# Self attention of a decoder layer: the products of exponents and values issued two key blocks at a time, with 16 slots for exponents

## The chip, the core and the metric

The kernel runs on one core of a Trainium2 chip. Its metric is the device time of one execution in microseconds; lower is better. The core has TensorE (PE in the profile; PEld is its weight load), VectorE (DVE), ScalarE (ACT), GpSimd (POOL) and SyncE (SP), which issues most transfers here. TensorE writes its results to PSUM, which has eight banks of 128 partitions by 512 words of fp32; a semaphore count tells another engine that a tile is ready, or that a bank is free again.

## What is computed

One decoder layer of a transformer on x with 4 sequences of 1024 tokens and 256 features: self attention, cross attention to 77 context rows, and a gated feed-forward network, each behind a layer norm and with a residual sum. The change touches self attention alone, 16 heads of 16 features with a causal mask:

```python
Qt = jnp.einsum('bqhf,hfg->bqhg', Q, W_cross)
scores_cross = jnp.einsum('bqhd,bkhd->bhqk', Qt, K)
K_mixed = jnp.einsum('hfg,bkhg->bkhf', M, K)
scores_conv = jnp.einsum('bqhf,bkhf->bhqk', Q, K_mixed)
scores = (gt * scores_cross + (1.0 - gt) * scores_conv) * scale
scores = jnp.where(causal[None, None], scores, -jnp.inf)
attn = jax.nn.softmax(scores, axis=-1)
out = jnp.einsum('bhqk,bkhd->bqhd', attn, V).reshape(b, s, H * hd)
```

## The kernel before

The stages follow one another: projections to q, k and v (to about 160 us), self attention (to about 646 us), its output projection and the query projection of cross attention, cross attention, and the feed-forward part (from about 900 us).

Self attention takes 16 groups, each of four heads of one sequence (HG is 4). In each group three kinds of work run on TensorE:

- **Maxima.** Scores with queries on partitions go into one of three PSUM banks (MXB), and VectorE reduces each tile to the largest value of each query. `ring` lists 38 such tiles and two small transposes: t0, which turns the maxima of the first half of the queries (place 15 of the ring), and t1, which turns those of the second half (place 39). These two write only 32 partitions. VectorE copies their result to a row, and a transfer adds it to the operands of the score tiles. The maxima of group g + 1 are made while the scores of group g are. In the text, r with a number is a place of the ring; r15 and r39 are called t15 and t39.
- **Scores.** With keys on partitions, in one of three other banks (STB). ScalarE takes the exponent of each tile and writes it to `prob`, a ring of NPS slots of 512 columns fp32. There are 38 such units in a group (NST), s0 to s37.
- **Products.** Exponents times values, fp32, for 128 keys (a key block) at a time: a set of four matmuls, one for each head, each from 128 partitions to 17 columns of the array (16 features and the sum of exponents). The profile has two records for each of these matmuls, so a set is x8. The sets are p0 to p11: p0 to p3 for the first 512 queries (4, 4, 2 and 1 score units; 512, 384, 256 and 128 query columns), p4 to p11 for the second 512 (five sets of 512 columns, then 384, 256 and 128). The first half accumulates in bank 6, the second in bank 7 (PVB).

The order of all this on TensorE is the list `plan`, made once from a few rules and the same in each group: a set is placed LAG = 3 score units behind the last unit that it needs; a set that would come behind s37 is placed in the next group's plan, with -1 (p10 behind s1 and p11 behind s2, for the group before). The maxima of the next group are spread evenly between the scores from s3 on. With t39 and r0 placed behind s3, the order before in one group is:

```
s0 s1 p10 s2 p11 s3 t39 r0 s4 r1 s5 r2 s6 p0 r3 s7 r4 s8 r5 s9 r6 s10 p1 r7 s11 r8 r9
s12 p2 r10 s13 p3 r11 s14 r12 s15 r13 s16 r14 s17 p4 t15 s18 r16 s19 r17 s20 r18 r19
s21 p5 r20 s22 r21 s23 r22 s24 r23 s25 p6 r24 s26 r25 s27 r26 s28 r27 s29 p7 r28 r29
s30 r30 s31 r31 s32 r32 s33 p8 r33 s34 r34 s35 r35 s36 r36 s37 p9 r37 r38
```

What waits for what: a score tile for the exponent three units back (`s_ex`, its bank); a tile of maxima for VectorE's work three places back (`s_mxe`); a product set for the exponent of its last unit (`s_ex`); an exponent for the product that frees its slot in `prob` (`s_pv`, against NPS); the copy of the first half's output for p3 and of the second's for p11 (`s_pv`), the first sets of a half (p0, p4) for the copy that frees their bank (`s_u`). VectorE works strictly in the order of the ring; behind the reduce of r10 and of r38 it has the two or three small operations that split the maxima into two bf16 parts (`parts_of_max`). In groups 5, 9 and 13 it also has `shares`, divisions for the sequence that is done, between r38 and t39. In the last group there are no maxima to make; the first steps of the next stage (`EARLY`) stand between its score units.

Of the kernel before, what the change touches and what calls it, by code (L numbers as in the profile page):

```python
# [23 lines left out]
def need(eng, semaphore, count):  # L24

    if count > 0:
        eng.wait_ge(semaphore, count)


def program(nc, x, ctx_t, mask_t, Wq, bq, Wk_t, bk, Wv_t, bv, Wo_t, bo, W_cross, shift_w, gate,  # L30
# [41 lines left out]
    with root:  # L72
# [505 lines left out]
        def self_plan():  # L578

            mx_units, st_units, sets = [], [], []  # L580
            for half in range(2):
                for r in range(4):
                    if half:
                        mx_units += [(half, 1, r, h, 1, 0, 512, False) for h in range(HG)]
                    hb = HG // (r + 1)
                    mx_units += [(half, 2 * half, r, h, hb, half * 512, (r + 1) * P, True)
                                 for h in range(0, HG, hb)]
            for half in range(2):
                for kt in range(4 * half + 4):
                    diag = kt >= 4 * half  # L590
                    q0 = (kt % 4) * P if diag else 0
                    n = 512 - q0
                    hb = max(1, (512 // n) // 2 * 2)
                    first = len(st_units)
                    st_units += [(half, kt, h, hb, q0, n, diag) for h in range(0, HG, hb)]
                    sets.append((half, kt, first, len(st_units), kt == 0, kt == 4 * half + 3, q0, n, hb))
            return mx_units, st_units, sets

        mx_units, st_units, sets = self_plan()
        NST = len(st_units)  # L600
        n_half = sum(1 for m in mx_units if m[0] == 0)
        half_end = [max(s[3] for s in sets if s[0] == h) for h in range(2)]
        ring = [("m", i) for i in range(len(mx_units))]
        ring.insert(n_half + 4, ("t", 0))
        ring.append(("t", 1))
        NMX = len(ring)
        NPS, LAG, LATE = 12, 3, 3
        MXB, STB, PVB = (0, 1, 2), (3, 4, 5), (6, 7)
        NMB, NSB = len(MXB), len(STB)

        plan, at = [], 0
        for u in range(NST):
            plan.append(("s", u, 0))
            plan += [("p", s, -1) for s, x in enumerate(sets) if x[3] - 1 == NST + u - LAG]
            plan += [("p", s, 0) for s, x in enumerate(sets) if x[3] - 1 == u - LAG]
            if u == LATE:
                plan.append(("r", NMX - 1, 0))
            upto = max(0, u - LATE + 1) * (NMX - 1) // (NST - LATE)
            plan += [("r", n, 1) for n in range(at, upto)]
            at = upto  # L620
# [161 lines left out]
        def self_tensor(t, first):  # L782
            def maxima(g, n):
                i, N = g % GB, g * NMX + n
                kind, m = ring[n]
                dst = bank[MXB[N % NMB]]
                if n == 0:
                    t.wait_ge(ld[i], 16 * NLD * (g // GB + 1))
                need(t, s_mxe, N + 1 - NMB)
                if kind == "t":  # L790
                    t.wait_ge(s_mt, 2 * g + m + 1)
                    nc.tensor.transpose(dst[0:32, 0:P // 2].bitcast(BF16),
                                        mt[:, m].rearrange("p t m -> p (t m)"), identb[:]).then_inc(s_mxf, 1)
                    return
                half, k, r, h0, hb, k0, w, diag = mx_units[m]
                for h in range(hb):
                    mm = nc.tensor.matmul(dst[:, h * w:(h + 1) * w],  # L797
                                          stq[i][0:R, half, h0 + h, r * P:(r + 1) * P],
                                          stk[i][0:R, h0 + h, k0:k0 + w],
                                          start=(h == 0), stop=not diag, skip_group_check=True)  # L800
                if diag:
                    mm = nc.tensor.matmul(dst[:, 0:hb * w].rearrange("p (h w) -> p h w", h=hb)[:, :, w - P:w],  # L802
                                          identb[:], tri_q[:, 0:hb], start=False, stop=True, skip_group_check=True)
                mm.then_inc(s_mxf, 1)

            def scores(g, u):
                i, U = g % GB, g * NST + u
                half, kt, h0, hb, q0, n, diag = st_units[u]
                if u == 0 or u == half_end[0]:
                    t.wait_ge(md[g % 2][half], 32 * (g // 2 + 1))  # L810
                need(t, s_ex, U + 1 - NSB)
                dst = bank[STB[U % NSB]]
                for h in range(hb):
                    mm = nc.tensor.matmul(dst[:, h * n:(h + 1) * n],  # L814
                                          stk[i][0:RM, h0 + h, kt * P:(kt + 1) * P], stq[i][0:RM, half, h0 + h, q0:q0 + n],
                                          start=(h == 0), stop=not diag, skip_group_check=True)
                if diag:
                    mm = nc.tensor.matmul(dst[:, 0:hb * n].rearrange("p (h n) -> p h n", h=hb)[:, :, 0:P],  # L818
                                          identb[:], tri_k[:, 0:hb], start=False, stop=True, skip_group_check=True)
                mm.then_inc(s_st, 1)  # L820

            def products(g, s):
                half, kt, first, end, fresh, last, q0, n, hb = sets[s]
                if fresh:
                    need(t, s_u, 2 * g + half - 1)
                t.wait_ge(s_ex, g * NST + end)
                for h in range(HG):
                    mm = nc.tensor.matmul(bank[PVB[half]][h * VW:h * VW + VC, q0:512], va[g % GB][:, kt, :, h],  # L828
                                          prob[:, (g * NST + first + h // hb) % NPS, (h % hb) * n:(h % hb + 1) * n],
                                          start=fresh, stop=last)  # L830
                mm.then_inc(s_pv, end - first)

            if first:
                for n in range(NMX - 1):
                    maxima(0, n)
                return

            t.wait_ge(s_set, GB)
            for g in range(G):
                for what, which, ahead in plan:  # L840
                    if g == G - 1 and what == "s" and which in EARLY:
                        if which == min(EARLY):
                            t.wait_ge(s_mxe, G * NMX)
                        EARLY[which](t)
                    if what == "s":
                        scores(g, which)
                    elif what == "p" and g + ahead >= 0:
                        products(g + ahead, which)
                    elif what == "r" and g + ahead < G:
                        maxima(g + ahead, which)  # L850
            for s, x in enumerate(sets):
                if x[3] - 1 > NST - 1 - LAG:
                    products(G - 1, s)


# [778 lines left out]
        with nc.Block() as block:  # L1634
# [26 lines left out]
            @block.tensor  # L1661
            def _(t):
                qkv_tensor(t)
                arrive(t)
                self_tensor(t, True)
                t.wait_ge(s_phase, 5)
                self_tensor(t, False)
# [177 lines left out]
```

## Time and profile before

| | us |
|---|---|
| median of three runs | 1145.98 (1141.55 to 1146.23) |
| the profiled execution | 1145.35 |
| its span, first to last instruction | 1143.6 |
| TensorE busy | 1044.8 |
| VectorE busy | 750.0 |
| ScalarE busy | 573.4 |
| TensorE busy within 165 to 646 us (481 us) | 478.15 |

The page of the profile gives busy time by engine, groups of instructions and releasers; the timeline gives single instructions or merged stretches in order. The end of a matmul record is modelled: it contains a tail that lies under the next one, so distances between starts tell more than durations. "Idle" in brackets behind a row is the time that the engine stood before it, and what ended it.

### The profile page before, as it was taken

The numbers are of one execution on the slowest core, as the hardware profiler recorded it, in microseconds if no ns is written. First come the engines' busy times: TensorE is split into PE (matmuls) and PEld (weight loads), VectorE is DVE, ScalarE is ACT, GpSimd is POOL, SyncE is SP. The second block draws the span as 40 slices with busy tenths as digits, with TensorE's granted clock in tenths as the row PEclk, the third lists the DMA queues.
The fourth block names the chain that finished last, engine by engine and source line by source line (L and its number), as shares of the span: only waits on it lengthen the run. The fifth ranks groups of instructions, "written<-read, shape, count | busy, mean of one in ns | idle before, by whom it ended". The sixth has DMA issues, their size and how long they took to land. (4 is left out here: it accounts for less than half of the span.)

```text
span 1143.6 us, 19037 instructions
## 1 busy us (share of the span) xinstructions
PE 1044.8 (91%) x7092; PEld 602.9 (53%) x7092; DVE 750.0 (66%) x1603; ACT 573.4 (50%) x1043; POOL 230.8 (20%) x192
## 2 busy tenths in 40 slices
PE   2889789999999999999999878898599899999997
PEld 2777234444444444444444455444243588888886
DVE  5997877777888878877785266555254355555552
ACT  1454146667767767667676549356256311111110
POOL 6654630000000000000000057200100133333331
PEclk9999679999999999999999998899699899999999
DMA  7279833433334444444110166666653201111101
GB/s 242 103 228 262 225 59 70 75 76 71 75 61 87 89 85 87 89 88 85 40 62 23 59 192 185 145 140 144 150 134 99 99 18 47 47 57 56 56 20 37
DMA packets 89636, 113.48 MB, mean 99 GB/s; under 512 B 13819, under 2 KB 74747, under 8 KB 88008
## 3 DMA queue, kind: packets, MB, share of 16 engines
q1 hardware_dynamic: 85896, 107.25, 37.6%
q10 hardware_dynamic: 3648, 5.02, 2.2%
q8 instruction: 56, 0.92, 0.4%
q14 instruction: 36, 0.29, 0.1%
HBM read 66.26 MB, written 45.45 MB: 98 GB/s over the span
## 5 line engine op out<-in xcount | busy, mean ns | idle before, releaser
L774 ACT ACTIVATE prob<-bank 128x512 f32<-128x512 f32 (+1 forms) x608 | 329.3, 575 | 184.8 <-PE bank L818 106.0
L726 DVE TENSOR_REDUCE pm<-bank 128x1 f32<-128x512 f32 (+3 forms) x608 | 364.6, 656 | 83.8 <-PE bank L802 63.7
L797 PE MATMUL bank<-stk,stq 96*128 96x512 bf16 (+3 forms) x768 | 227.3, 340 | 8.4 <-DVE pm L726 4.1
L814 PE MATMUL bank<-stq,stk 98*128 98x512 bf16 (+3 forms) x768 | 222.9, 329 | 0.9 <-ACT prob L774 0.8
L828 PE MATMUL bank<-prob,va 128*17 128x512 f32 (+3 forms) x1536 | 164.5, 501 | 0.0
L797 PEld LDWEIGHTS bank<-stk,stq 96*128 96x128 bf16 x768 | 70.2, 99 | 160.3 <-DVE pm L726 115.6
L1550 ACT ACTIVATE e_sg<-bank 128x512 f32<-128x512 f32 x48 | 28.7, 598 | 188.4 <-PE bank L132 188.4
L1308 ACT ACTIVATE xprob<-bank 80x512 f32<-80x512 f32 x128 | 73.8, 593 | 87.1 <-PE bank L1345 83.8
L957 POOL TENSOR_TENSOR c_rstd<-c_ve,mhalf 128x4 f32<-128x4 f32 x8 | 8.1, 1008 | 508.0 <-DVE c_ve L125 508.0
L814 PEld LDWEIGHTS bank<-stq,stk 98*128 98x128 bf16 x768 | 69.4, 98 | 56.9 <-issue 12.4
L1270 DVE TENSOR_REDUCE xpm<-bank 128x4 f32<-128x320 f32 x128 | 60.5, 489 | 53.8 <-PE bank L1331 52.1
L802 PE MATMUL bank<-tri_q,identb 128*128 128x128 bf16 (+2 forms) x352 | 88.6, 252 | 0.0
L818 PE MATMUL bank<-tri_k,identb 128*128 128x128 bf16 (+2 forms) x352 | 86.5, 246 | 0.0
L132 PE MATMUL bank<-e_xnt,wg 128*128 128x512 f32 x288 | 76.7, 402 | 1.4 <-DVE e_xnt L1511 1.4
L1479 POOL TENSOR_TENSOR e_ht<-e_hf,e_ht 128x512 fp32r<-128x512 f32 x48 | 62.4, 1300 | 73.1 <-DVE e_ht L1506 73.1
L132 PE MATMUL bank<-e_xnt,wu 128*128 128x512 f32 x288 | 73.8, 392 | 0.0
L132 PE MATMUL bank<-wd,e_ht 128*128 128x256 f32 x576 | 70.5, 283 | 3.2 <-POOL e_ht L1479 3.2
L132 PEld LDWEIGHTS bank<-wd,e_ht 128*128 128x128 f32 x576 | 70.1, 192 | 4.2 <-POOL e_ht L1479 3.6
L1504 DVE TENSOR_TENSOR e_hf<-bank,e_sg 128x512 f32<-128x512 f32 x48 | 33.1, 690 | 50.6 <-ACT e_sg L1550 50.6
L828 PEld LDWEIGHTS bank<-prob,va 128*17 128x17 f32 x1536 | 31.4, 117 | 57.0 <-ACT prob L774 33.8
L132 PEld LDWEIGHTS bank<-e_xnt,wg 128*128 128x128 f32 x288 | 54.2, 191 | 12.7 <-DVE e_xnt L1511 1.8
L132 PEld LDWEIGHTS bank<-e_xnt,wu 128*128 128x128 f32 x288 | 54.6, 190 | 11.7
(173 smaller groups left out, 1388.6 us busy)
## 6 DMA issues: line engine op xcount, KB each, us to landing
qk<-a_parts SPq DMA_DIRECT2D x32, 384.0 KB, 4.1
od<-u_out SPq DMA_DIRECT2D x16, 512.0 KB, 3.2
oin<-od SPq DMA_DIRECT2D x32, 256.0 KB
od<-xu SPq DMA_DIRECT2D x16, 512.0 KB, 2.7
xq<-c_parts SPq DMA_DIRECT2D x16, 384.0 KB, 3.1
xstq<-xq SPq DMA_DIRECT2D x32, 192.0 KB, 3.9
stq<-qk SPq DMA_DIRECT2D x28, 192.0 KB, 4.9
stk<-qk SPq DMA_DIRECT2D x14, 384.0 KB, 7.3
```

Of the source, the lines that this page charges most:

```text
L132: mm = nc.tensor.matmul(dst, a[:, i], b[:, j], start=(n == 0), stop=(n == 3 * len(terms) - 1))
L726: nc.vector.tensor_reduce(pm[:, k, h0:h0 + hb, r], src[:, 0:hb * w].rearrange("p (h w) -> p h w", h=hb), AX, ALU.max).then_inc(s_mxe, 1)
L774: nc.scalar.activation(prob[:, U % NPS, 0:hb * n], bank[STB[U % NSB]][:, 0:hb * n], ACT.Exp).then_inc(s_ex, 1)
L797: mm = nc.tensor.matmul(dst[:, h * w:(h + 1) * w], stq[i][0:R, half, h0 + h, r * P:(r + 1) * P], stk[i][0:R, h0 + h, k0:k0 + w], start=(h ...
L802: mm = nc.tensor.matmul(dst[:, 0:hb * w].rearrange("p (h w) -> p h w", h=hb)[:, :, w - P:w], identb[:], tri_q[:, 0:hb], start=False, stop= ...
L814: mm = nc.tensor.matmul(dst[:, h * n:(h + 1) * n], stk[i][0:RM, h0 + h, kt * P:(kt + 1) * P], stq[i][0:RM, half, h0 + h, q0:q0 + n], start ...
L818: mm = nc.tensor.matmul(dst[:, 0:hb * n].rearrange("p (h n) -> p h n", h=hb)[:, :, 0:P], identb[:], tri_k[:, 0:hb], start=False, stop=True ...
L828: mm = nc.tensor.matmul(bank[PVB[half]][h * VW:h * VW + VC, q0:512], va[g % GB][:, kt, :, h], prob[:, (g * NST + first + h // hb) % NPS, ( ...
L1270: nc.vector.tensor_reduce(xpm[:, half, :, r], src[:, 0:HG * SK].rearrange("p (h w) -> p h w", h=HG), AX, ALU.max).then_inc(xs_mxe, 1)
L1308: nc.scalar.activation(xprob[:, U % NPS2], bank[STB[U % NSB]][0:SK, :], ACT.Exp).then_inc(xs_ex, 1)
L1479: nc.gpsimd.tensor_tensor(ht[:, c % 2, 1, h], hf[:, h % 2], ht[:, c % 2, 0, h].bitcast(F32), ALU.subtract).then_inc(es_hl, 1)
L1504: nc.vector.tensor_tensor(hf[:, h % 2], bank[5 + 2 * (h % 2)][:], sg[:, h % 2], ALU.mult).then_inc(es_h, 1)
```

## The change

`joint_end` holds, for each product set, the end of the score units of the second set of its pair: (0, 1), (2, 3), (4, 5), (6, 7), (8, 9), (10, 11). Both sets of a pair are now placed three units behind that end, so they stand next to each other. `prob` has 16 slots in place of 12; it takes 32 KB of each partition where it took 24.

```diff
         half_end = [max(s[3] for s in sets if s[0] == h) for h in range(2)]
+        joint_end = [sets[s - s % 2 + 1][3] for s in range(len(sets))]
...
-        NPS, LAG, LATE = 12, 3, 3
+        NPS, LAG, LATE = 16, 3, 3
...
             plan.append(("s", u, 0))
-            plan += [("p", s, -1) for s, x in enumerate(sets) if x[3] - 1 == NST + u - LAG]
-            plan += [("p", s, 0) for s, x in enumerate(sets) if x[3] - 1 == u - LAG]
+            plan += [("p", s, -1) for s in range(len(sets)) if joint_end[s] - 1 == NST + u - LAG]
+            plan += [("p", s, 0) for s in range(len(sets)) if joint_end[s] - 1 == u - LAG]
...
-            for s, x in enumerate(sets):
-                if x[3] - 1 > NST - 1 - LAG:
+            for s in range(len(sets)):
+                if joint_end[s] - 1 > NST - 1 - LAG:
                     products(G - 1, s)
```

In the plan p10 moves behind s2, p0 behind s10, p2 behind s13, p4 behind s21, p6 behind s29 and p8 behind s37; the order of the scores and of the maxima stays. All lines behind the first one added have a number higher by 1.

The rows below are TensorE's, in group 1 (`stq1`), beside the maxima of group 2 (`stq2`). bank0 to 2 take maxima, bank3 to 5 scores, bank6 and 7 products. First around s13, the end of the first half, before:

```order
L814 MATMUL bank5<-stq1,stk1 128x512 [waits b_ex]
L828 MATMUL bank6<-prob,va1 17x256 [waits b_ex]
L828 MATMUL bank6<-prob,va1 17x256 x3
L797 MATMUL bank0<-stk2,stq2 128x512 [waits b_mxe]
L802 MATMUL bank0<-tri_q,identb 128x128
L814 MATMUL bank3<-stq1,stk1 128x512 [waits b_ex]
L828 MATMUL bank6<-prob,va1 17x128 [waits b_ex]
L828 MATMUL bank6<-prob,va1 17x128 x3
```

The same place now:

```order
L815 MATMUL bank5<-stq1,stk1 128x512 [waits b_ex]
L798 MATMUL bank0<-stk2,stq2 128x512 [waits b_mxe]
L803 MATMUL bank0<-tri_q,identb 128x128
L815 MATMUL bank3<-stq1,stk1 128x512 [waits b_ex]
L829 MATMUL bank6<-prob,va1 17x256 [waits b_ex]
L829 MATMUL bank6<-prob,va1 17x256 x3
L829 MATMUL bank6<-prob,va1 17x128 [waits b_ex]
L829 MATMUL bank6<-prob,va1 17x128 x3
```

p2 has moved past r10 and s13 to stand before p3. Next the stretch from s17 to s18 before, with p4 and the transpose t15:

```order
L814 MATMUL bank4<-stq1,stk1 128x512 [waits b_ex]
L828 MATMUL bank7<-prob,va1 17x512 [waits b_ex,b_u]
L828 MATMUL bank7<-prob,va1 17x512 x3
L792 MATMUL bank2<-identb,mt 32x128 [waits b_mt,b_mxe]
L814 MATMUL bank5<-stq1,stk1 128x512 [waits b_ex]
```

The same place now, from r14 on:

```order
L798 MATMUL bank1<-stk2,stq2 128x512 [waits b_mxe]
L815 MATMUL bank4<-stq1,stk1 128x512 [waits b_ex]
L793 MATMUL bank2<-identb,mt 32x128 [waits b_mt,b_mxe]
L815 MATMUL bank5<-stq1,stk1 128x512 [waits b_ex]
L798 MATMUL bank0<-stk2,stq2 128x128 [waits b_mxe]
```

p4 no longer stands between s17 and t15. It is found behind s21, where p5 was alone before:

```order
L798 MATMUL bank0<-stk2,stq2 128x512 [waits b_mxe]
L815 MATMUL bank5<-stq1,stk1 128x512 [waits b_ex]
L829 MATMUL bank7<-prob,va1 17x512 [waits b_ex,b_u]
L829 MATMUL bank7<-prob,va1 17x512 x3
L829 MATMUL bank7<-prob,va1 17x512 [waits b_ex]
L829 MATMUL bank7<-prob,va1 17x512 x3
L798 MATMUL bank1<-stk2,stq2 128x512 [waits b_mxe]
L815 MATMUL bank3<-stq1,stk1 128x512 [waits b_ex]
```

From p2 and p3 on, eight score units and nine places of the ring stand in a row before the next product, where there were four.

## Rows read from the trace of the kernel before

**Rows 1.** The page, part 1: busy us, share of the span, instructions by engine.

```profile
PE 1044.8 (91%) x7092; PEld 602.9 (53%) x7092; DVE 750.0 (66%) x1603; ACT 573.4 (50%) x1043; POOL 230.8 (20%) x192
```

**Rows 2.** Stretches: us, busy of PE, PEld, DVE, ACT, POOL, clock, DMA share, GB/s.

```profile
400.45:430.91 30.46, 30.46 (x241) 13.08 (x239) 24.03 (x45) 21.37 (x40) 0.00 (x0) 1.00 0.43 80
...
165.00:646.00 481.00, 478.15 (x3694) 204.90 (x3693) 370.90 (x712) 333.77 (x627) 2.42 (x4) 1.00 0.35 69
```

**Rows 3.** Groups by shape, 165 to 600 us: busy us, mean ns, idle before, releasers.

```profile
L726 DVE TENSOR_REDUCE pm<-bank 128x1 f32<-128x512 f32 x345 | 219.1, 684 | 44.8 <-PE bank L802 25.7 <-PE bank L797 18.3
```

**Rows 4.** Timeline of TensorE, 405 to 417 us: start, us, instruction, count.

```profile
405.81 0.85 PE L828 MATMUL bank<-prob,va 128*17 128x384 f32 x8
406.60 0.39 PE L797 MATMUL bank<-stk,stq 96*128 96x512 bf16 x1
...
406.89 0.38 PE L814 MATMUL bank<-stq,stk 98*128 98x512 bf16 x1
...
407.97 0.64 PE L828 MATMUL bank<-prob,va 128*17 128x256 f32 x8
408.55 0.39 PE L797 MATMUL bank<-stk,stq 96*128 96x512 bf16 x1
...
409.14 0.43 PE L828 MATMUL bank<-prob,va 128*17 128x128 f32 x8
409.50 0.39 PE L797 MATMUL bank<-stk,stq 96*128 96x512 bf16 x1
...
411.04 0.38 PE L814 MATMUL bank<-stq,stk 98*128 98x512 bf16 x1
411.35 1.07 PE L828 MATMUL bank<-prob,va 128*17 128x512 f32 x8
412.24 0.22 PE L792 MATMUL bank<-identb,mt 128*32 128x128 bf16 x1
412.39 0.39 PE L814 MATMUL bank<-stq,stk 98*128 98x512 bf16 x1
...
413.71 0.68 PE L797 MATMUL bank<-stk,stq 96*128 96x512 bf16 x2
...
414.55 1.07 PE L828 MATMUL bank<-prob,va 128*17 128x512 f32 x8
415.55 0.39 PE L797 MATMUL bank<-stk,stq 96*128 96x512 bf16 x1
...
415.99 0.38 PE L797 MATMUL bank<-stk,stq 96*128 96x256 bf16 x2
...
416.33 0.38 PE L814 MATMUL bank<-stq,stk 98*128 98x512 bf16 x1
```

**Rows 5.** Timeline of TensorE, the last group's p9, p10 and p11.

```profile
644.07 1.50 PE L828 MATMUL bank<-prob,va 128*17 128x384 f32 x24
```

**Rows 6.** Timeline of VectorE, 410 to 425 us: reduces merged where they overlap.

```profile
410.06 2.48 DVE L726 TENSOR_REDUCE pm<-bank 128x1 f32<-128x512 f32 x4
...
413.26 2.48 DVE L726 TENSOR_REDUCE pm<-bank 128x4 f32<-128x512 f32 x4 [0.53 <-PE bank L802]
415.97 2.48 DVE L726 TENSOR_REDUCE pm<-bank 128x1 f32<-128x512 f32 x4 [0.23 <-PE bank L797]
...
422.08 2.09 DVE L726 TENSOR_REDUCE pm<-bank 128x1 f32<-128x384 f32 x4 [0.68 <-PE bank L802]
```

**Rows 7.** Timeline behind t39 of a group with shares, both engines.

```profile
340.65 0.20 DVE L723 COPY mrow<-bank 32x128 bf16<-32x128 bf16 x1
...
340.91 0.39 PE L797 MATMUL bank<-stk,stq 96*128 96x256 bf16 x2 [0.17 <-DVE mrow L723]
```

**Rows 8.** Waits, 165 to 600 us: waiting, releaser, us in total, times, longest.

```profile
PEld bank L797 <- DVE pm L726: 93.3, 143, 0.8
```

**Rows 9.** Timeline in the last group.

```profile
629.08 2.06 ACT L774 ACTIVATE prob<-bank 128x512 f32<-128x512 f32 x4 [0.91 <-PE bank L814]
...
629.73 0.39 PE L814 MATMUL bank<-stq,stk 98*128 98x512 bf16 x1 [0.26 <-ACT prob L774]
```

## The prediction

> **What bounds the kernel now.** I read the page first: TensorE is busy for 91% of the span [rows 1]. The stage that the change touches, self attention, lies at 165 to 646 us. There TensorE is busy for 478 of 481 us, at a granted clock of 1.00, the upper level of 2.4 GHz [rows 2]. One head group takes 30.46 us, all of it busy TensorE, beside 24.0 us of VectorE and 21.4 us of ScalarE [rows 2]. So between groups 1 and 14 an instruction that TensorE is spared is time gained, as long as the other two keep up. How tightly they keep up decides this case: VectorE uses 79% of the time, and it frees only three banks. I call a tile of maxima r (numbered 0 to 39 in its ring), a tile of scores s (0 to 37), a product set p (0 to 11).
>
> Next I read TensorE's instructions in order of time [rows 4]. Between two products every r and s of 512 columns follows its neighbour by 0.22 us: seven steps from 409.50 to 411.04. A product set is different. Its 32-row outputs use a quarter of the array per head, and the way in and the way out cost something:
> - In: s at 411.04, product at 411.35. That is 0.31 where a step of 0.22 was due, so 0.09.
> - Out: a set of 512 columns at 414.55 is followed by a 128-row tile at 415.55, 1.00 later. The set at 411.35 is followed by the small transpose (t, 32 rows wide) after only 0.89. The way out is 0.11 dearer to a full tile.
>
> **The price of a join.** The trace holds a run of adjacent sets already: p9, p10 and p11 of the last group, 24 records from 644.07, busy 1.50 us [rows 5]. Alone, the same three sets take 0.79, 0.57 and 0.36 us from start to next start (405.81 to 406.60, 407.97 to 408.55, 409.14 to 409.50) [rows 4], 1.72 in sum. A lone set's modelled end lies 0.07 behind the next start (0.43 against 0.36), so the run is worth 1.43. Two joins save 0.29 of the ways out, 0.145 each, and one way in each, 0.09. A join is worth 0.24 us, and no gap shows inside the run for loading the next set's values.
>
> **Which joins count.** There are six in a group, but not six gains. Before, t15 (ring place 15) follows p4 directly and shares its narrow shape: 0.89 into it, 0.15 out of it (412.24 to 412.39) [rows 4]. Now p4 stands beside p5, and t15 alone pays a way in (0.09) and a way out: joining p4 and p5 gives what t15 loses, net 0. The trace shows this first; the Trainium skill, TensorEngine Tiling (Array Packing), Key Properties, says the same in general, that changing the tiling mode, not just the tile, drains the engine. Counting all six joins alike would put the sum about 3.5 us lower. So five joins: 5 x 0.24 = 1.20 us a group.
>
> **What the joins take away.** A lone product gave VectorE and ScalarE 1.0 us to empty their banks after each four tiles. Now eight tiles stand in a row. An r may start only when the reduce three places back has ended. A reduce of 512 columns lasts 0.68 [rows 3], they follow each other every 0.60 ((2.48 - 0.68) / 3), those of 384 columns every 0.47 ((2.09 - 0.68) / 3) [rows 6], and the release takes 0.06: the first reduce from 413.26 ends at about 413.95, and the second r of the pair at 413.71 starts at 413.71 + 0.68 - 0.38 = 414.01 [rows 4, 6]. A reduce starts 0.42 after its r at the earliest (415.55 to 415.97) [rows 4, 6]. So r(n) may start 0.74 after the start of reduce n-3. That wait already occurs once a group, 0.08 us at r19. I carry it through the new order by hand. From p5's end (0) to p6, with 0.22 for a tile, 0.33 for one of two 256-column heads (415.99 to 416.33) and 0.06 more for a 128-column mask product (406.60 to 406.89 is 0.29, 0.01 of it the first step behind a run) [rows 4]:
> - r20 at 0, r21 at 0.45, r22 at 1.00, r23 at 1.55, r24 at 1.98; their reduces at 0.43, 1.03, 1.63, 2.23, 2.83. No wait.
> - r25 at 2.42 (free from 2.37), reduce 3.43. r26 would start at 2.92 and is free at 2.97: wait 0.05. r27 would start at 3.46, free at 3.57: wait 0.10. Together 0.15, and then p6.
>
> The same count from p7 to p8 (r28 to r36): r34 would start at 2.50 and is free at 2.57, r35 3.12 and 3.17, in sum 0.12. From p3 to p4 VectorE begins late, since the two operations that split the first half's maxima stand between the reduces of r10 and r11. There r14 waits 0.08, t15 0.06, r16 0.21 and r19 its old 0.08: 0.35 more than before. From r0 to p0 no wait, but only 0.19 to spare. In sum 0.62 us a group. ScalarE needs no such wait: four exponents of 512 columns take 2.06 us, about 0.5 each [rows 9], and where the r tiles are dear a score tile comes every 0.5 to 0.6; it is busy for 21.4 of 30.46 us.
>
> The ring of exponents costs nothing: with 16 slots the exponent of unit u waits for the product of unit u - 16. A pair spans at most eight units and is issued three units behind its last, so the oldest unit without its product is never more than ten behind; even 12 slots would wait for nothing. The stores, the loads of the next group and both output copies wait for p3, p11 and the group's end, which keep their places.
>
> **The sum**, against the profiled execution's 1145.35 us:
> - Groups 1 to 14: 14 x (1.20 - 0.62) = 8.1 gained. Group 0 has no p10 and p11 before it: 0.96 - 0.62 = 0.3 gained.
> - In three groups (the ones with shares) VectorE's divisions stand before the copy of t39: it comes at 340.65, and r2 waits for it (340.91) [rows 7]. TensorE now comes to t39 earlier by 0.24 and lacks the pause of p0 behind r2: r2 waits 0.24 more, r3 to r5 0.05, 0.16 and 0.04. 3 x 0.5 = 1.5 lost.
> - The last group has no maxima; TensorE waits for exponents there, 0.26 us at 629.73 [rows 9]. What a join saves it waits for. I take 0; bounds are 1.2 gained (all five joins) and 1.2 lost (a run of two sets, 1.9 us, and 0.4 to the next exponent, outlasts three score tiles of 0.5 us each by some 0.8, of which a lone run's own cost is saved; three times 0.4).
> - Everything later keeps its order and moves up by the same amount.
>
> 1145.35 - 8.1 - 0.3 + 1.5 = **1138.4 us**. The median of the runs shown is 0.6 higher than this execution, which I leave out as scatter.
>
> **Rivals.**
> - *No new waits: 1127.6.* All joins count: 14 x 1.20 + 0.96 = 17.8. For it: TensorE's loads of r wait for VectorE 93 us in sum [rows 8], but most of it stands under running products, and the matmuls lost nothing. Against it: r14 already starts only 0.02 us after it may (one step before 411.04, so 410.82; the reduce of r11 began at 410.06, plus 0.74 is 410.80) [rows 4, 6], and one wait exists. Chance 0.12.
> - *The waits are larger, the gain is gone: 1142 to 1147.* The conditions above are sharp to a few hundredths each; if each of the eight waits is 0.07 longer, 0.56 a group is lost more and 1145.8 results. The Trainium skill, TensorEngine Tiling (Array Packing), PSUM Bottleneck, warns of this kind of limit: a faster TensorE does not empty PSUM faster. Chance 0.17.
> - *Slower: VectorE becomes the bound.* The mechanism is its bank ring in the three stretches of eight tiles. If the reduces came every 0.66 us there and not 0.60 (their busy time alone is 0.68), the count gives waits of 0.40, 0.39 and 0.83 more than before's: 1.62 a group against 1.20 saved, 14 x 0.42 + 1.5 more = 7 lost, 1152.8. It decides against the change from 0.635 on. Against it: every packed row shows 0.60. Chance 0.05.
> - *The joins aren't worth 0.24.* If a second 512-column set stalls on its own loads where the short ones did not, up to 0.1 each: 1145 at most. Contained in the second case; the joined run of rows 5 speaks against it.
>
> **Numbers.** Forecast 1135 to 1142, chance 0.66, with 1138.4 in it; the rivals 0.12, 0.17 and 0.05. A measurement of this kernel tells about 0.5%, 5.7 us: faster by that means below 1140.2. The forecast lies there with four fifths of its chance, and the first rival wholly: 0.65. Slower by over 0.5% (above 1151.7): 0.04. Between: 0.31. The range 1130 to 1145 leaves out the first rival, the slower one and the edge of the second.
>
> **What would show it.** A group should take 29.9 us in place of 30.46. A joined pair of 512-column sets should be busy about 1.93 us with no gap, and its way in and out unchanged. t15 should stand alone, with 0.31 before and 0.16 behind it. Waits of r on the reduce should appear at r14, t15, r16, r26, r27, r34 and r35. VectorE should idle over 1 us behind each joined run where it idled 0.5 to 0.8. If the group takes 29.3 us, the waits are my error; if a gap stands inside the joined run, the price of a join is; if the prediction fails with both right, it is the last group.

## The result, and the profile after

| | before | after |
|---|---|---|
| median of 15 runs each | 1145.33 us (1141.05 to 1148.57) | 1138.12 us (1133.67 to 1141.15) |
| profiled execution, span | 1145.35, 1143.6 | 1138.45, 1136.7 |

The ratio is 0.9939, with a 95% interval of 0.9926 to 0.9952: 7.2 us faster, 0.6%. The forecast of 1138.4 is 0.3 above the median. That it came this close is partly luck: in the profiled execution one term of the sum was 1.3 us off, the stage began 0.8 us earlier, and a later stage gave 2.3 us back. All three come up below.

The page's first part answers to [rows 1]:

```profile
PE 1031.2 (91%) x7092; PEld 607.5 (53%) x7092; DVE 737.0 (65%) x1603; ACT 561.9 (49%) x1043; POOL 230.8 (20%) x192
```

The counts of instructions are the same, and TensorE is busy for 13.6 us less (1044.8 to 1031.2). That is more than the time gained. Of the 13.6, 8.2 lie in groups 1 to 14, which got 6.8 us shorter, and 1.8 lie behind self attention, in a part that took 2.3 us longer. Busy time is not the price of a join.

These stretches (the columns are those of [rows 2]) are group 0, a plain group, and the last group up to the end of its products. A group goes from its first score tile, s0, to the next group's:

```profile
145.86:182.15 36.29, 31.66 (x225) 14.33 (x223) 28.65 (x47) 20.41 (x39) 6.74 (x3) 0.86 0.18 32
...
421.92:451.79 29.87, 29.82 (x241) 13.54 (x240) 23.39 (x46) 20.54 (x40) 0.00 (x0) 1.00 0.45 84
...
602.75:636.07 33.32, 30.96 (x223) 14.39 (x221) 13.09 (x38) 19.80 (x40) 2.42 (x4) 1.00 0.06 20
```

The same for the first and last group of the kernel before, which the rows ahead of the prediction don't show:

```profile
146.70:184.56 37.86, 33.27 (x224) 14.13 (x223) 29.23 (x47) 20.91 (x39) 6.75 (x3) 0.83 0.13 26
...
611.99:645.30 33.31, 31.39 (x222) 13.96 (x221) 13.09 (x38) 20.33 (x40) 2.42 (x4) 1.00 0.06 20
```

A plain group went from 30.46 [rows 2] to 29.87. Group 0 went from 37.86 to 36.29. The last group did not move. The three groups with shares went from 30.79 to 30.68 each.

TensorE's timeline of a plain group, from p0 on, answers to [rows 4]. Its columns are start, us, instruction and count:

```profile
428.27 1.71 PE L829 MATMUL bank<-prob,va 128*17 128x512 f32 x16
...
433.67 0.38 PE L815 MATMUL bank<-stq,stk 98*128 98x512 bf16 x1
...
433.95 0.39 PE L798 MATMUL bank<-stk,stq 96*128 96x512 bf16 x1
434.18 0.38 PE L815 MATMUL bank<-stq,stk 98*128 98x512 bf16 x1
434.55 0.23 PE L793 MATMUL bank<-identb,mt 128*32 128x128 bf16 x1
434.71 0.39 PE L815 MATMUL bank<-stq,stk 98*128 98x512 bf16 x1
...
435.15 0.40 PE L798 MATMUL bank<-stk,stq 96*128 96x128 bf16 x4
...
436.26 0.68 PE L798 MATMUL bank<-stk,stq 96*128 96x512 bf16 x2
...
436.78 0.38 PE L815 MATMUL bank<-stq,stk 98*128 98x512 bf16 x1
437.09 1.93 PE L829 MATMUL bank<-prob,va 128*17 128x512 f32 x16
438.95 0.39 PE L798 MATMUL bank<-stk,stq 96*128 96x512 bf16 x1
```

The reader is to see three things. First, p4 and p5 are one row of 16 records (two for each of their eight matmuls), 1.93 us, entered 0.31 after the score tile before (436.78 to 437.09) and left after 1.86. There is no gap in it. Two sets of 512 columns apart took 1.07 each and 1.00 to the next start [rows 4]. Second, t15 stands alone: it starts 0.37 behind its score tile (0.31 for the way in, 0.06 of wait) and the next follows 0.16 later. Third, the ways into and out of the other five runs are as before.

VectorE's timeline answers to [rows 6]. The brackets give its idle time ahead:

```profile
430.40 2.48 DVE L727 TENSOR_REDUCE pm<-bank 128x1 f32<-128x512 f32 x4 [1.84 <-PE bank L803]
...
433.22 2.47 DVE L727 TENSOR_REDUCE pm<-bank 128x1 f32<-128x512 f32 x4
...
435.80 2.48 DVE L727 TENSOR_REDUCE pm<-bank 128x4 f32<-128x512 f32 x4
...
439.38 4.74 DVE L727 TENSOR_REDUCE pm<-bank 128x1 f32<-128x512 f32 x8 [1.09 <-PE bank L798]
...
445.41 5.07 DVE L727 TENSOR_REDUCE pm<-bank 128x1 f32<-128x384 f32 x9 [1.29 <-PE bank L803]
```

VectorE now idles 1.1 to 1.8 us behind a joined run, and then reduces eight or nine tiles without a pause. There TensorE catches up with it and waits. Before, it had 0.2 to 0.7 us of idle time behind each single set, and four reduces in a row [rows 6].

### The profile page after: what moved, and what is told of

Same layout as the page of the kernel before. It is cut to its first block and busy times, and to the rows that moved or that the text cites. A ratio compares the mean times of both kernels' runs of the same rounds, so it can differ in the third digit from the quotient of the medians.

```text
span 1136.7 us, 19033 instructions
## 1 busy us (share of the span) xinstructions
PE 1031.2 (91%) x7092; PEld 607.5 (53%) x7092; DVE 737.0 (65%) x1603; ACT 561.9 (49%) x1043; POOL 230.8 (20%) x192
## 5 line engine op out<-in xcount | busy, mean ns | idle before, releaser
L727 DVE TENSOR_REDUCE pm<-bank 128x1 f32<-128x512 f32 (+3 forms) x608 | 356.4, 653 | 88.0 <-PE bank L803 71.7
L775 ACT ACTIVATE prob<-bank 128x512 f32<-128x512 f32 (+1 forms) x608 | 317.5, 584 | 187.1 <-PE bank L819 102.9
L829 PE MATMUL bank<-prob,va 128*17 128x512 f32 (+3 forms) x1536 | 143.8, 492 | 0.0
L829 PEld LDWEIGHTS bank<-prob,va 128*17 128x17 f32 x1536 | 40.3, 113 | 71.9 <-issue 52.3
L132 PEld LDWEIGHTS bank<-e_xnt,wu 128*128 128x128 f32 x288 | 54.6, 190 | 11.6
```

The source lines that it names most:

```text
L132: mm = nc.tensor.matmul(dst, a[:, i], b[:, j], start=(n == 0), stop=(n == 3 * len(terms) - 1))
L727: nc.vector.tensor_reduce(pm[:, k, h0:h0 + hb, r], src[:, 0:hb * w].rearrange("p (h w) -> p h w", h=hb), AX, ALU.max).then_inc(s_mxe, 1)
L775: nc.scalar.activation(prob[:, U % NPS, 0:hb * n], bank[STB[U % NSB]][:, 0:hb * n], ACT.Exp).then_inc(s_ex, 1)
```

## The experiments

In all of them a plain group is compared from its s0 to the next group's s0, as above. All ratios are against the kernel before on the same chip. A "narrow stretch" is a run of product sets, or a 32-row transpose, with tiles of the full width ahead and behind.

**e1: the ring of 12 slots again.**

```diff
-        NPS, LAG, LATE = 16, 3, 3
+        NPS, LAG, LATE = 12, 3, 3
```

> The changed kernel with 12 slots for exponents in place of 16; the pairs stay joined. My theory: the ring's length plays no part (the oldest unit without its product is at most ten behind), so 1138 us, ratio 0.994 to the kernel before, a group of 29.87 us as with 16 slots. Rival, that the longer ring carries part of the gain or is needed: exponents then wait for products, a group is longer by 0.1 us or more, 1140 us or above.

Measured: 1139.06 us, ratio 0.9941 [0.9921, 0.9961]. The plain group takes 29.88. The larger ring does nothing that can be seen; the gain is the order's.

**e2: only p4 and p5 joined.** This is the one join that the prediction counted at net zero.

```diff
-        joint_end = [sets[s - s % 2 + 1][3] for s in range(len(sets))]
+        joint_end = [sets[5][3] if s == 4 else x[3] for s, x in enumerate(sets)]
```

> Only p4 and p5 are joined, the other sets stand alone as before. My theory: this join saves nothing, since t15 shared p4's narrow shape before and now pays its own way in and out; what is left is the waits of r14, t15 and r16 on VectorE, about 0.2 us a group, so 14 x 0.2 = 3 us slower than before, about 1148, a group of 30.6 to 30.7 us. Rival, every join saves 0.24: 30.2 plus the waits, 30.4 at most, no slower than before.

```profile
429.59:460.30 30.71, 30.31 (x237) 13.17 (x239) 23.95 (x46) 21.05 (x40) 0.00 (x0) 1.00 0.39 81
```

Measured: 1151.51 us, ratio 1.0051 [1.0031, 1.0071]. The group takes 30.71, as expected: this join earns nothing and brings waits of 0.25. Counting this join at 0.24 like the others would have said 30.2, or 30.5 with the waits. The total missed: the median is 3.5 above what was expected. The profiled execution took 1148.83, and in it the last group took 2.4 more than before, against less time elsewhere; how the other executions spent their 2.7 more isn't on record. In that last group the granted clock fell. TensorE and the stretches of e2's last group (windows show the clock as the third column from the end):

```profile
630.89 0.37 PE L923 MATMUL bank<-rd,sel 48*128 48x512 bf16 x1 [1.84 <-DVE oin L929]
...
632.81 3.30 PE L829 MATMUL bank<-prob,va 128*17 128x512 f32 x16
```

```profile
632.50:634.50 2.00, 2.00 (x10) 0.34 (x13) 0.00 (x0) 1.18 (x3) 0.00 (x0) 0.50 0.05 12
634.50:636.00 1.50, 1.50 (x12) 0.17 (x4) 0.00 (x0) 0.00 (x0) 0.00 (x0) 0.62 0.00 0
```

TensorE waited 1.84 us for VectorE; 1.9 us later the same joined run of p4 and p5 took 3.30 us at a granted clock of 0.50, the lower level of 1.2 GHz, instead of 1.93. In the changed kernel the wait at this place was 1.41 (0.84 in the kernel before), and the run went at 1.00:

```profile
618.07 0.37 PE L923 MATMUL bank<-rd,sel 48*128 48x512 bf16 x1 [1.41 <-DVE oin L929]
...
619.77 1.93 PE L829 MATMUL bank<-prob,va 128*17 128x512 f32 x16
```

The fall is not tied to 1.84 alone. Of the twelve traces, the longest wait for VectorE ahead of p4 in the last group was 1.41 or more in seven: the clock fell behind it in e2, e5, e6 and e10, and did not in the changed kernel, e1 and e3. In the other five (before, e4, e7, e8, e9) it was at most 0.85, and no fall came in this group. What decides among the seven is open.

**e3 and e4: the reduce made cheap, in both orders.** Both kernels take the maxima over the first half of each tile's columns and scale the exponents by 0.02. TensorE's work is untouched.

```diff
-                                        src[:, 0:hb * w].rearrange("p (h w) -> p h w", h=hb),
+                                        src[:, 0:hb * w].rearrange("p (h w) -> p h w", h=hb)[:, :, 0:w // 2],
...
-                                         ACT.Exp).then_inc(s_ex, 1)
+                                         ACT.Exp, scale=0.02).then_inc(s_ex, 1)
```

The changed order (e3):

> The changed kernel with each maximum taken over half of its tile's columns only (the other half is left out, and the exponents are scaled by 0.02 so that they stay finite); VectorE's reduces get shorter by some 0.27 us and come every 0.33 instead of 0.60. My theory: the waits of r on VectorE (0.63 us a group) go and the joins show their full price: a group of 29.25 us, 14 x 0.62 + 1.5 = 10 us below the changed kernel, about 1128. Rival, the missing gain is not VectorE's (a joined run is slower than its parts, or the release costs it): a group stays above 29.6, 1135 or more.

The order before (e4):

> The kernel before with the same halved maxima and scaled exponents (half of each tile's columns is left out of the maximum). My theory: it has only one wait of 0.08 us a group to lose, and 0.33 in three groups, so a group of 30.38 and 1143 us; the difference of 15 to 16 us to the changed kernel with the same edit is then the full price of five joins a group (1.2 us) and group 0. Rival, shorter reduces help both alike: both kernels fall by the same amount and stay 7 us apart.

The reduces of e3, grouped by shape, and a plain group of e3:

```profile
L727 DVE TENSOR_REDUCE pm<-bank 128x1 f32<-128x256 f32 x346 | 143.0, 424 | 106.1 <-PE bank L803 65.7 <-PE bank L798 35.0
```

```profile
408.66:437.94 29.28, 29.02 (x237) 13.96 (x239) 16.50 (x46) 20.39 (x40) 0.00 (x0) 1.00 0.43 85
```

A plain group of e4:

```profile
420.25:450.61 30.36, 30.01 (x237) 13.23 (x239) 16.54 (x46) 21.38 (x40) 0.00 (x0) 1.00 0.40 82
```

Measured: e3 1120.94 us, 0.9773 [0.9732, 0.9814]; e4 1138.95 us, 0.9951 [0.9932, 0.9971]. A reduce now has a mean of 424 ns instead of 684 [rows 3]. With it, the old order gains 0.1 a group (30.46 to 30.36) and the new one 0.59 (29.87 to 29.28). This is the test of the main reason: the same six joins are worth 0.59 us with the real reduces and 1.08 with cheap ones. The prediction said 0.58 and 1.20. The waits on VectorE are what eats most of the rest. Behind the 0.12 that is missing stands a new wait of 0.14, once in each of e3's plain groups and not found in e4: a score tile follows its r by 0.36 where 0.22 is due, and its weight load waits for ScalarE's exponent:

```profile
422.21 0.38 PE L798 MATMUL bank<-stk,stq 96*128 96x512 bf16 x1
422.56 0.10 PEld L815 LDWEIGHTS bank<-stq,stk 98*128 98x128 bf16 x1 [0.47 <-ACT prob L775]
422.57 0.39 PE L815 MATMUL bank<-stq,stk 98*128 98x512 bf16 x1
```

With these 0.14 the joins come to 1.22, which is 0.24 for each of the five. So ScalarE is the next limit behind VectorE. Between the medians lie 18.0 us where 15 to 16 were expected (14.2 between the profiled executions), and both totals fell further than expected. The stage starts 11 us earlier in both, since the first maxima lie ahead of it, and its first group takes 3 to 4 us longer.

**e5: t15 moved beside the joined p4 and p5.** If the narrow transpose shares their ways in and out, a stretch is saved; but the splitting operations then stand elsewhere in VectorE's row.

```diff
-        ring.insert(n_half + 4, ("t", 0))
+        ring.insert(n_half + 9, ("t", 0))
```

> The changed kernel with the transpose of the first half's maxima moved from ring place 15 to place 20, directly behind the joined p4 and p5, so that it shares their narrow shape again. By the price of a join alone this saves 0.24 us a group, 14 x 0.24 = 3.4 us: 1135. By my count of the waits on VectorE it does not: the light tile no longer sits among the dear ones, nine full reduces stand in a row between p3 and p4, and the waits there grow by about 0.45. So a group of 30.05 us in place of 29.87, and about 1140.

```profile
424.53:454.56 30.03, 29.82 (x240) 13.55 (x239) 23.40 (x46) 20.53 (x40) 0.00 (x0) 1.00 0.45 83
```

Measured: 1142.72 us, 0.9981 [0.996, 1.0002]. The plain groups take 30.03 to 30.04: a narrow stretch fewer than the changed kernel, and yet 0.17 slower. Fewer stretches alone are not the aim. The total is 2.7 above what was expected; in the profiled execution the last group took 1.2 more than in the changed kernel (below).

**e6: all joins but p0 with p1.**

```diff
-        joint_end = [sets[s - s % 2 + 1][3] for s in range(len(sets))]
+        joint_end = [x[3] if s < 2 else sets[s - s % 2 + 1][3] for s, x in enumerate(sets)]
```

> The changed kernel with p0 and p1 apart again, as before; the other pairs stay joined. My theory: a group loses one join, 29.87 + 0.24 = 30.11 us; the three groups with shares get p0's pause back and stay at 30.7; in group 0 p0 runs at the lower clock again (in the trace of before it took 1.85 us where 1.00 is usual), which gives back 1.1 to 1.5 us. Sum 11 x 0.24 + 1.3 = 4 us above the changed kernel, 1142. Rival, group 0's extra gain in the changed kernel is scatter of the start: group 0 stays at 36.3 to 36.6.

```profile
425.20:455.32 30.12, 30.07 (x241) 13.41 (x240) 23.67 (x46) 20.82 (x40) 0.00 (x0) 1.00 0.40 83
...
146.00:183.67 37.67, 33.04 (x225) 14.26 (x223) 28.79 (x47) 20.46 (x39) 6.74 (x3) 0.83 0.14 28
```

Measured: 1143.25 us, 0.9982 [0.9961, 1.0002]. The group rises by 0.25, one join without any new wait of its own, as the count of the stretch r0 to p0 said. Group 0 rises by 1.4 to 37.67, nearly all of what it had gained. The last group took 1.3 more, with a fall of the clock as in e2. The 1.4 of group 0 points to where the missed term sits; its working is below.

**e9: two runs of four sets.** p0 to p3 are one run and p8 to p11 another; p4 with p5 and p6 with p7 stay pairs.

```diff
-        joint_end = [sets[s - s % 2 + 1][3] for s in range(len(sets))]
+        joint_end = [sets[(3, s - s % 2 + 1, 11)[(s > 3) + (s > 7)]][3] for s in range(len(sets))]
```

> The changed kernel with longer runs: p0 to p3 in one run and p8 to p11 in one run, p4 with p5 and p6 with p7 as now; maxima stay evenly spread. Two more joins a group, 0.48 us; VectorE idles in the longer runs, but the stretch from p3 to p4 begins with VectorE at rest. By my count the waits stay at about 0.65 us: a group of 29.35 us, 1145 - 14 x 1.1 = 1130. Rival, longer runs starve VectorE for good and the waits grow by as much as the joins save: 29.9 and 1138.

```profile
415.55:444.91 29.36, 29.34 (x240) 13.82 (x239) 23.40 (x46) 20.36 (x41) 0.00 (x0) 1.00 0.43 85
```

Measured: 1128.49 us, 0.987 [0.983, 0.9911]. The group takes 29.36, as expected: two more joins, and waits that did not grow.

**e7: runs and maxima tiles placed together.** The tables give, for each maxima tile and each set, the score unit behind which it is issued (from 38 on it is in the next group). They group the sets where the ring has slack and bring the maxima tiles closer to what VectorE can take: 0, 1, 2 or 3 behind a unit instead of about one.

```diff
-        NPS, LAG, LATE = 12, 3, 3
+        NPS, LAG, LATE = 16, 3, 3
...
+        TILES_AT = (2, 3, 4, 5, 6, 8, 8, 9, 10, 12, 12, 12, 14, 15, 17, 17, 18, 19, 19, 20, 21, 22, 22, 23, 24, 25, 27, 28, 28, 29, 31, 32, 32, 33, 33, 35, 36, 37, 37)
+        SETS_AT = (13, 13, 13, 13, 20, 24, 33, 33, 40, 40, 40, 40)
...
-            plan += [("p", s, -1) for s, x in enumerate(sets) if x[3] - 1 == NST + u - LAG]
-            plan += [("p", s, 0) for s, x in enumerate(sets) if x[3] - 1 == u - LAG]
-            if u == LATE:
+            plan += [("p", s, -1) for s in range(len(sets)) if SETS_AT[s] - NST == u]
+            plan += [("p", s, 0) for s in range(len(sets)) if SETS_AT[s] == u]
+            if u == 2:
...
-            plan += [("r", n, 1) for n in range(at, upto)]
+            plan += [("r", n, 1) for n in range(NMX - 1) if TILES_AT[n] == u]
```

> A version meant to beat both: the order is written as a table. Runs are p0 to p3 behind s13, p4 alone, p5 alone, p6 with p7 behind s33, p8 to p11 behind s2 of the next group with the transpose of the second half's maxima in the same run; the maxima are placed so that no tile waits for VectorE: two in a row behind a run or an expensive stretch, one or none where VectorE is behind. By the row durations no wait is left and the ways in and out fall to 5 runs and one lone transpose: a group of 28.75 us, 14 x 1.7 = 24 us below the kernel before, 1121. If the waits on VectorE are not the only cost of bunching, it stays above 29.3 us a group, 1130 or more.

```profile
410.78:439.46 28.68, 28.68 (x240) 13.85 (x239) 23.63 (x47) 20.11 (x41) 0.00 (x0) 1.00 0.44 87
```

```profile
440.38 2.36 PE L828 MATMUL bank<-prob,va 128*17 128x512 f32 x32
442.56 0.22 PE L792 MATMUL bank<-identb,mt 128*32 128x128 bf16 x1
442.72 0.40 PE L797 MATMUL bank<-stk,stq 96*128 96x128 bf16 x4
```

Measured: 1118.62 us, 0.977 [0.9728, 0.9812]: some 27 us faster than before, and some 20 faster than the change. p8 to p11 and t39 share one way in and one way out (the second fence): t39 starts 2.18 behind the run's start, and the next full tile 0.16 later.

**e8 and e10: its two halves apart.** e8 keeps e7's table of sets with the even spacing of the maxima tiles; t39 stands behind unit 3 again.

```diff
-        TILES_AT = (2, 3, 4, 5, 6, 8, 8, 9, 10, 12, 12, 12, 14, ...
+        TILES_AT = (3, 4, 5, 6, 7, 8, 9, 10, 11, 11, 12, 13, 14, ...
...
-            if u == 2:
+            if u == 3:
```

> The version of the table with its product runs alone (p0 to p3 behind s13, p4, p5, p6 with p7 behind s33, p8 to p11 behind s2); the maxima are spread evenly again, as in the changed kernel, and the transpose of the second half's maxima comes behind s3. By my count waits on VectorE of about 0.65 us a group come back, above all 0.4 at r29 (ten tiles stand in a row from p5 to p6), and one way in and out: a group of 29.6 us, about 1131, 12 us above the table. If the runs alone made the table's gain, it stays at 28.8 us and 1120.

e10 keeps e7's table of tiles with the pairs of the changed kernel.

```diff
-        SETS_AT = (13, 13, 13, 13, 20, 24, 33, 33, 40, 40, 40, 40)
+        SETS_AT = (10, 10, 13, 13, 21, 21, 29, 29, 37, 37, 40, 40)
```

> The other half: the changed kernel's pairs with the table's places for the maxima. Those places were made for other runs; by my count they fit the pairs worse than the even spread does, waits of 1.4 us a group (r28 0.36, r34 0.30, t39 0.29): 30.3 us a group, and 31.3 in the three groups with shares, about 1144. If early and doubled maxima were good in themselves, this would lie below the changed kernel's 1138.

A plain group of e8, then of e10:

```profile
417.18:446.74 29.56, 29.36 (x240) 13.80 (x239) 23.50 (x47) 20.52 (x41) 0.00 (x0) 1.00 0.46 85
```

```profile
428.62:459.03 30.41, 29.85 (x240) 13.64 (x239) 23.71 (x46) 20.35 (x40) 0.00 (x0) 1.00 0.40 82
```

Measured: e8 1129.52 us, 0.9854 [0.9833, 0.9874]; e10 1148.82 us, 1.0028 [1.0015, 1.004]. The groups came out as expected, within 0.1. e10's total did not (1144 expected): its first group takes 38.36, and its last 35.66 at a mean granted clock of 0.95. The tiles' table alone is a loss of 0.53 a group against the changed kernel, the sets' table alone a gain of 0.30; both together gain 1.19. It is no sum of two effects, because the waits belong to the pair.

**All orders in one account.** The kernel before has 13 narrow stretches in a group (12 sets, t15 beside p4, t39 alone), and waits of 0.08. So a group with k stretches would take 30.38 - 0.24 x (13 - k) without any wait, and the rest is waiting. The last column is another measure of the same thing, from the trace alone: a step between two of TensorE's starts is compared with the shortest step between the same two shapes in any of the twelve traces, and what it takes more, from 0.03 on, is summed up (steps inside a product set are left out).

| kernel | stretches | without waits | measured | waits | waits, from steps |
|---|---|---|---|---|---|
| before | 13 | 30.38 | 30.46 | 0.08 | 0.08 |
| e2, p4 with p5 alone | 13 | 30.38 | 30.71 | 0.33 | 0.33 |
| e6, all but p0 with p1 | 9 | 29.42 | 30.12 | 0.70 | 0.69 |
| after | 8 | 29.18 | 29.87 | 0.69 | 0.67 |
| e5, t15 beside p5 | 7 | 28.94 | 30.04 | 1.10 | 1.04 |
| e10, tiles' table | 7 | 28.94 | 30.40 | 1.46 | 1.45 |
| e8, sets' table | 7 | 28.94 | 29.57 | 0.63 | 0.63 |
| e9, two runs of four | 6 | 28.70 | 29.36 | 0.66 | 0.64 |
| e7, both | 6 | 28.70 | 28.68 | -0.02 | 0 |

The column "waits" is what is left over, so it holds errors of the 0.24 too (with 0.22, e7 would have -0.16, which no wait can be). That the steps give the same waits within 0.06 bears out both the 0.24 and the count of stretches. The count by hand before each run gave the group's time within 0.1 in all eight of the new orders.

## Why the prediction was right, and where it was not

**The price of a join: right.** The joined 512-column pair was forecast at 1.93 busy without a gap, and is 1.93. The rival on this (a stall of the second set on its own loads) shows in no run, up to the four sets of e7 at 2.36 us. The rule cited of the Trainium skill, TensorEngine Tiling (Array Packing), Key Properties, that a change of mode drains the engine, agrees with the trace where it counted: t15 lost its cheap way in when it lost p4 (0.31 and a wait instead of sharing p4's), and e2 shows that this join earned nothing.

**The waits: right, in place and size.** The count said 0.62 more a group. In this group r14 starts 0.07 late (0.28 behind its score tile, where 0.22 is due), t15 0.06 late, r16 0.21, r19 0.08 as before, r26 0.05, r27 0.10, r34 0.07 and r35 0.04: 0.60 more than before. The forecast list was the same seven places and r19. e3 is the experiment behind it. "No new waits: 1127.6" needed 29.3 a group, and e3 shows that number only with the reduce cheapened. "The waits are larger" needed 0.07 more at each of eight places, and they came out 0.02 below the count in sum. (Its own time should read 1146.2, not 1145.8: 14 x 0.56 are 7.8 on top of 1138.4.) "VectorE becomes the bound" needed reduces that follow each other more slowly than every 0.60; the four in the row at 435.80 take 2.48, as before, which is one every 0.60, and the eight from 439.38 come at no slower pace: (4.74 - 0.68) / 7 = 0.58.

**The list of waits misleads here.** Over 165 to 600 us, the changed kernel's largest entries between these two engines are these:

```profile
DVE pm L727 <- PE bank L803: 65.4, 54, 1.8
...
PEld bank L798 <- DVE pm L727: 64.3, 172, 0.8
```

TensorE's loads wait for VectorE 64 us in sum, less than the 93 of before [rows 8], though the real loss grew by 0.6 a group. The load waits ahead of its product, under products that still run. The loss is found only in the steps between the starts of products, and the prediction was right to set the 93 us aside.

**Groups with shares: right.** Forecast: 0.08 gained a group net; measured 0.11.

**The ring: right.** e1 shows 12 slots to be as good.

**Group 0: the term that was mis-sized.** The prediction gave it 0.96 - 0.62 = 0.3, by the prices of a plain group; it gained 1.57. The sum overlooked the granted clock at the start of the stage. It read the clock from 165 us on, and the group's s0 stands at 146.70 already. In group 0 the granted clock is 0.50 at first. Before, p0 ran under it, at 1.92 us instead of 1.07. The kernel before, then the changed one; first TensorE's products, then the stretches around the rise:

```profile
157.35 1.92 PE L828 MATMUL bank<-prob,va 128*17 128x512 f32 x8
```

```profile
157.00:159.80 2.80, 2.80 (x13) 0.55 (x12) 0.69 (x1) 0.49 (x1) 0.00 (x0) 0.50 0.00 0
159.80:163.00 3.20, 3.20 (x31) 1.81 (x29) 2.19 (x4) 2.24 (x4) 0.00 (x0) 1.00 0.00 0
```

```profile
158.64 1.71 PE L829 MATMUL bank<-prob,va 128*17 128x512 f32 x16
```

```profile
153.50:156.30 2.80, 2.80 (x14) 1.64 (x13) 1.50 (x3) 0.98 (x2) 0.00 (x0) 0.51 0.02 3
156.30:163.00 6.70, 6.70 (x67) 3.43 (x66) 4.79 (x9) 4.37 (x8) 0.00 (x0) 1.00 0.01 2
```

In the changed kernel p0 waits for p1, and by then the clock has risen: from 10.4 us into the group, against 13.1 before. e6, which undoes this join alone, has both back, p0 at the lower level and the late rise:

```profile
156.64 1.92 PE L829 MATMUL bank<-prob,va 128*17 128x512 f32 x8
```

```profile
156.00:158.90 2.90, 2.90 (x15) 0.57 (x14) 0.69 (x1) 0.66 (x2) 0.00 (x0) 0.50 0.00 0
158.90:165.00 6.10, 6.10 (x59) 3.25 (x58) 4.77 (x9) 3.93 (x7) 0.00 (x0) 1.00 0.00 0
```

p0 at the lower level costs 0.85 (a step of 1.85 instead of 1.00); that and the join's own 0.24 are 1.1 of the 1.4 that e6 gave back. In e2, where p0 is alone too, the rise fell into p0 and it took 1.45. Group 0 takes 37.86, 37.67 and 37.43 with p0 alone (before, e6, e2), and 36.29, 36.60 and 36.35 with the changed kernel's order there (after, e1, e5). So p0's place goes with 0.8 to 1.6 us in this group.

That the order also moves the rise of the clock is not shown. It comes 11.6 to 13.1 us into the group in the first three and 10.4 to 11.0 in the other three, but at 13.2 in e7 and 13.4 in e10, which also keep p0 from being alone. And the clock of single executions differs before the orders do. This is a stretch ahead of the stage, in which both kernels have the same work, before and then after:

```profile
125.60:128.90 3.30, 2.97 (x9) 0.74 (x7) 3.27 (x5) 0.00 (x0) 0.95 (x1) 0.50 0.10 35
```

```profile
125.60:128.90 3.30, 1.84 (x7) 0.40 (x5) 3.27 (x5) 0.00 (x0) 1.80 (x1) 1.00 0.02 8
```

How much of the 1.57 is the order's and how much is one execution's therefore stays open.

**The last group: the value was right, the bounds were not.** It kept its 33.3 us up to its last products, as forecast. But the prediction bounded it at 1.2 either way, and from s0 to the end of the last product it took 33.59 in before and after, 33.5 to 33.6 in e1, e3, e4, e7 and e8, 34.82 in e5, 34.9 in e6, 35.47 in e9, 35.66 in e10 and 36.03 in e2. In e2, e5, e6 and e10 the run of p4 and p5 took 3.30, 2.94, 2.99 and 3.49 us instead of 1.93. e5:

```profile
623.61 2.94 PE L829 MATMUL bank<-prob,va 128*17 128x512 f32 x16
```

No term of the prediction held a fall of the clock, and with one the last group was 1.2 to 2.4 longer. The changed kernel has the long wait of 1.41 behind which four of seven traces show the fall; that its profiled execution is one of the other three is luck as far as is known. In e9 no fall shows and the group is still 1.9 longer. One wait of 1.02 us is part of that: at 600.12 a score tile waits for the transfer that adds the maxima to its operands, which it does in none of the other traces. The rest was not taken apart.

**"Everything later moves up by the same amount": not in the profiled execution.** Self attention ended 9.2 us earlier, 0.84 of it from an earlier start of the stage, ahead of anything that was changed. Then 2.3 came back: from the end of self attention to the end of the run it took 498.1 before and 500.4 after. In the ten experiments, whose code is the same there, the like stretch takes 496.6 to 503.5, so this is within the scatter of single executions. Sum of the steps on the profiled execution: 11 x 0.59 + 3 x 0.11 + 1.57 = 8.4 in the stage, 0.84 ahead of it, 2.3 back, 6.9 in all (1145.35 to 1138.45). The medians say 7.2.

## What to carry to other kernels

Read the way into and out of a narrow shape as steps between starts, price each stretch of narrow work once, and let what is narrow (small transposes too) share a stretch. Then carry the ring's release times through the new order by hand, tile by tile: an engine that is busy throughout loses its time in waits of a few hundredths of a microsecond, and grouping without moving the producers of the other engine's work gave back half or more of the gain here (joins 1.2, waits 0.6 a group), while planning both together gave all of it (e7). At the edges of a stage look at the granted clock of the very stretch before using prices from its middle.

## What the runs showed of the hardware that was not expected

- In the last group the clock fell to 0.50 after TensorE had waited 1.84 us (e2) and 1.41 us (e5, e6, e10), and did not after 1.41 us in the changed kernel, e1 and e3, nor in the five traces in which that wait was at most 0.85. One fall lengthened the run of p4 and p5 from 1.93 to 3.30 us.
- In the first group the moment of the rise moved between 156.3 us (after) and 159.8 (before). At 125.6 to 128.9 us the same work had been granted 1.00 in the one and 0.50 in the other, so the order of the work can't be named as its cause.
- Four sets, which load new weights for every matmul, still show no gap when they stand in a row: 32 records in 2.36 us (e7).
- With VectorE's reduces cheapened, the next engine to hold a tile back was ScalarE, by 0.14 us a group (e3).
